# A two-layer decoder on one core: the last mixture writes finished rows, pads are cleared once counts are known, masks move to GpSimd

## The chip, the cores and the metric

The kernel runs as one program on one core of a Trainium2 chip. The engines of the core are named as the profile names them: PE is TensorE (PEld its weight loads), DVE is VectorE, ACT is ScalarE, POOL is GpSimd, and SP is SyncE, which here only starts DMAs. The metric is the device time of one execution in microseconds (us); less is better.

## The reference

The input x is 4 batches of 512 tokens with 128 features; a context of 154 tokens comes per batch. Two layers of attention and mixture follow, each added to x:

```python
x = x + L0_attn(layernorm(x), ...)            # linear attention
x = x + L0_xattn(layernorm(x), ctx, masks)    # 16 heads over 154 keys, two masks
x = x + L0_ffn(layernorm(x), ...)             # mixture: 8 experts, 1 chosen per token
x = x + L1_attn(layernorm(x), ...)            # relative positions
x = x + L1_xattn(layernorm(x), ctx, ...)      # causal over the keys
x = x + L1_ffn(x, ...)                        # rotary attention, then the mixture below
```

The last of them ends in the mixture that the change is mostly about:

```python
h = x + attention(rmsnorm(x, g1), wq, wk, wv, wo)
xf = rmsnorm(h, g2)                            # 2048 tokens x 128
vals, idx = top_k(xf @ router_w + router_b, 2)
scores = softmax(vals)
oh = one_hot(idx, 8)
pos = cumsum(cumsum(oh, axis=0), axis=1)       # place in the expert's queue
emask = oh * (pos < 256)
tmask = sum(emask, -1)
m = max(einsum('tke,e->tk', emask, arange(8)), -1)   # ONE expert per token
y = (gelu((xf @ w2[m]) * (xf @ w1[m])) @ w3[m])      # hidden size 256
out = h + sum_k scores_k * (y if tmask_k > 0 else xf)
```

So every token goes through exactly one expert m, and its result is `(h + xf * cz) + y * cy` with two factors per token, cz and cy, which are known before any expert has run.

## The kernel before, in words

The stages are named A to G in the code: A, B and C are the first layer's attention, cross-attention and mixture, D, E and F the second layer's attentions, G the last mixture. A, B and the gate of C run batch by batch, then C's experts, then D, then E, F and the gate of G batch by batch, then G's experts. Each engine has its own list of instructions, written out by hand in that order; semaphores are the only order between engines.

**Start.** SP issues the loads of the constants in groups; `s_const[1]` says that the second group (masks among it) has landed. In batch 0 the DVE normalises x, then runs `dve_prepare` (L709 to 723): it waits for that group and makes the bf16 masks `xmask`, `amask`, `kmask`, `cpick` and `cmask` and the column `pcol`. Only then come the values of the cross-attention (L569) and, when PE has projected x (L338), the keys of the linear attention `kf` (L386 to L390), for which PE waits (L346). L320 (the bias), L355 and L315 follow on PE. The masks are first read at L410 on DVE. POOL meanwhile widens the context's keys and values (L618, L621). SP also fills the scratch `xs_d` with zeros (L2022, 12.1 MB), since a mixture's tiles may hold rows that no token was written to.

**A mixture.** Tokens are grouped by expert through DRAM. An indirect DMA of POOL writes each group of 128 tokens to rows of `xs_d` (`pool_G_send`, L1829), each expert having a region. From the counts, `dve_tiles` (L835 to 857) works out which 23 tiles of 128 rows are to be run (NS = 23), the expert of each (`expert4`) and its first row (`rows4`). Then, for each tile s of the last mixture: SP loads the tile (L1938, six buffers); PE transposes it (`flip`, L1841) and DVE copies the result (L1902); POOL copies the two first weights of the tile's expert into one of two buffers (L1955); PE runs eight matmuls (`hidden`, L1850); ACT copies one half (L1882), DVE multiplies the halves (L1909), ACT applies Gelu (L1889); PE runs the third weight (`result`, L1860); DVE copies y out of PSUM (L1922); SP stores it over the tile's rows in `xs_d` (L1945). An instruction that takes a tile number or address from a table reads it first into a register (`value_load`).

When all tiles are stored, POOL gathers the rows back into token order with 16 indirect DMAs (L1960), DVE adds `y * cy` to `h + xf * cz` per batch (L1926), and SP writes the batch to the output (L2048).

**Between D and E.** SP stores D's last results, waits for them (`sp_D_store`), loads `rot` (L2039) and then `sp_D1` loads E's input in 18 DMAs per batch (L1410, L1415, L1416), for which POOL waits (L1431).

## Time and profile before

| what | us |
|---|---|
| median of 3 runs | 1671.35 |
| lowest and highest | 1669.7 and 1675.36 |
| the profiled execution's own time | 1675.38 |
| its span (first to last record) | 1673.6 |
| busy PE / DVE / ACT / POOL | 1423.6 / 966.6 / 749.0 / 232.3 |
| chain that ended last: PE / DVE / SP's queue / DMA / POOL | 69% / 15% / 4% / 3% / 2% |

The page gives busy time of each engine over the whole span, and the "chain that ended last", which is followed back from the last instruction to what released it. PE holds most of that chain, but not at its two ends. In the last 28 us, from 1646 on, PE and ACT have no instruction at all, and in the first 46 us the cores' clock for PE, shown as a granted share of full speed (1.0 is 2.4 GHz, 0.5 is 1.2 GHz), goes from one level to the other and back. A timeline row has the start, the duration, the engine, the line, the operation and its tiles, how many were merged, and in brackets how long the engine was idle before it and what ended that.

### The profile page before, as it was taken

To read this page: it belongs to the slowest core of one execution; us is meant where nothing else is said; L and a number is where in the kernel's file an instruction comes from. 1 tells how busy PE (TensorE), PEld (TensorE's weight loads), DVE (VectorE), ACT (ScalarE), POOL (GpSimd) and SP (SyncE) were. 2 spreads that over 40 slices of the span, in tenths; PEclk is the share of its full clock that TensorE was granted. 3 is DMA by queue.
4 is the path that set the end of the run, shared out by engine and by line. 5 is a ranking of instruction groups with operands and counts; after the bars stand their busy time and mean duration, and the time that the engine had idled before them with its cause. 6 is when DMAs were issued, how large, how long until landed. Compare 5 with 4: busy or idle time off the path is not lost.

```text
span 1673.6 us, 43831 instructions
## 1 busy us (share of the span) xinstructions
PE 1423.6 (85%) x17681; PEld 878.2 (52%) x17681; DVE 966.6 (58%) x2541; ACT 749.0 (45%) x1927; POOL 232.3 (14%) x201
## 2 busy tenths in 40 slices
PE   4889888696499999999958999889989898999672
PEld 3343434393266666766633466346644564456462
DVE  4354635323477777777723676576665776477532
ACT  1323142251266666666613276327723672447431
POOL 1011120123030030200010200030002100120124
PEclk7989999797799999999978899999989998899897
DMA  9600000023230100100021000000000000000012
GB/s 327 264 17 1 17 1 7 17 58 98 77 140 4 26 19 10 35 4 16 4 76 43 1 2 2 5 7 2 2 5 7 2 2 1 7 1 1 6 55 70
DMA packets 62072, 60.07 MB, mean 36 GB/s; under 512 B 27952, under 2 KB 47024, under 8 KB 60720
## 3 DMA queue, kind: packets, MB, share of 16 engines
q1 hardware_dynamic: 59536, 53.04, 10.0%
q0 software_dynamic: 2048, 4.20, 0.9%
q8 instruction: 142, 2.33, 0.6%
q14 instruction: 58, 0.48, 0.1%
q10 hardware_dynamic: 288, 0.03, 0.0%
HBM read 32.73 MB, written 24.51 MB: 34 GB/s over the span
## 4 chain that ended last, share of the span: by engine, by line
PE 69%; DVE 15%; issue 4%; SPq 4%; DMA 3%; ACT 3%; POOL 2%; ACTq 0%; POOLq 0%; DVEq 0%
PE ps L1126 7%; PE ps L1514 6%; PE ps L1533 5%; PE ps L500 5%; PE ps L1547 4%; PE ps L1106 4%; PE ps L1116 4%; DVE arena L586 4%; PE ps L1147 4%; PE ps L258 4%; PE ps L1502 3%; PE ps L474 3%; PE ps L1161 2%; PE ps L1556 2%; PE ps L797 2%
## 5 line engine op out<-in xcount | busy, mean ns | idle before, releaser
L1259 DVE TENSOR_REDUCE nmax<-ps 128x1 f32<-128x512 f32 x256 | 166.8, 683 | 56.3 <-PE ps L1116 55.7
L1590 ACT ACTIVATE arena<-ps,arena 128x512 f32<-128x512 f32 (+3 forms) x256 | 135.5, 531 | 119.1 <-DVE arena L1650 112.9
L1650 DVE TENSOR_REDUCE arena<-ps 128x1 f32<-128x512 f32 (+3 forms) x256 | 124.3, 487 | 78.8 <-PE ps L1518 76.7
L1219 ACT ACTIVATE arena<-ps,nmax 128x512 f32<-128x512 f32 x172 | 119.0, 692 | 80.8 <-DVE nmax L1259 79.3
L1533 PE MATMUL ps<-sqc,arena 128*128 128x128 f32 x640 | 106.6, 287 | 20.0 <-DVE arena L1658 19.7
L586 DVE TENSOR_REDUCE arena<-ps 128x8 f32<-128x1232 f32 x64 | 89.2, 1438 | 40.3 <-PE ps L462 40.1
L258 PE MATMUL ps<-identb 128*128 128x512 bf16 x408 | 110.0, 430 | 1.4 <-DVE kcol L707 1.4
L1267 DVE COPY arena<-ps 128x512 f32<-128x512 f32 x128 | 88.0, 688 | 39.9 <-PE ps L1126 38.4
L1514 PE MATMUL ps<-arena 64*128 64x384 f32 (+3 forms) x512 | 106.2, 493 | 0.0
L1658 DVE TENSOR_SCALAR arena<-arena 128x512 f32<-128x512 f32 (+3 forms) x256 | 100.8, 394 | 9.1
L598 DVE RECIPROCAL arena<-ps 128x128 f32<-128x128 f32 x8 | 7.7, 959 | 160.4 <-PE ps L500 160.4
L1547 PE MATMUL ps<-arena 128*64 128x128 f32 x1280 | 99.0, 286 | 0.0
L1601 ACT COPY arena<-ps 128x512 f32<-128x512 f32 (+3 forms) x256 | 95.8, 431 | 4.0 <-PE ps L1533 3.9
L1126 PE MATMUL ps<-sqc,arena 128*128 128x128 f32 x688 | 94.9, 281 | 2.1 <-DVE arena L1267 0.9
L1533 PEld LDWEIGHTS ps<-sqc,arena 128*128 128x128 f32 x640 | 71.9, 142 | 46.1 <-issue 26.4
L1126 PEld LDWEIGHTS ps<-sqc,arena 128*128 128x128 f32 x688 | 74.2, 142 | 21.4 <-issue 15.5
L1229 ACT COPY arena<-ps 128x512 f32<-128x512 f32 x128 | 74.4, 581 | 16.4 <-PE ps L1126 16.4
L1547 PEld LDWEIGHTS ps<-arena 128*64 128x64 f32 x1280 | 68.8, 138 | 13.6 <-issue 1.7
L1116 PEld LDWEIGHTS ps<-rk,cw 64*128 64x128 f32 x512 | 43.9, 190 | 60.0 <-issue 55.3
L258 PEld LDWEIGHTS ps<-identb 128*128 128x128 bf16 x408 | 45.3, 111 | 56.6 <-issue 22.5
L1116 PE MATMUL ps<-rk,cw 64*128 64x168 f32 (+25 forms) x512 | 74.6, 411 | 0.0
L306 ACT ACTIVATE root<-var 128x4 f32<-128x4 f32 x32 | 6.6, 206 | 148.6 <-DVE var L288 126.3
(350 smaller groups left out, 2713.1 us busy)
## 6 DMA issues: line engine op xcount, KB each, us to landing
xs_d<-onehot SPq DMA_DIRECT2D x3, 3072.0 KB, 29.6
cw<-in_cw SPq DMA_DIRECT2D x2, 2048.0 KB, 13.4
rv<-in_rv SPq DMA_DIRECT2D x2, 1536.0 KB, 19.7
late<-in_gw SPq DMA_DIRECT2D x3, 1024.0 KB, 10.8
arena<-xs_d SPq DMA_DIRECT2D x46, 64.0 KB, 1.8
xs_d<-arena SPq DMA_DIRECT2D x46, 64.0 KB, 1.6
xs_d<-onehot SPq DMA_DIRECT2D x1, 2560.0 KB, 22.4
onehot<-q_s SPq DMA_DIRECT2D x96, 8.0 KB
```

The costliest lines, as they stand in the source:

```text
L258: nc.tensor.matmul(ps[:, FILL[k][1], :].rearrange("p (a n) -> p a n", a=NT), identb[:, :], identb[:, :].unsqueeze(1).to_broadcast([P, NT, ...
L586: nc.vector.tensor_reduce(top_x[:, i, :, 2 * hp:2 * hp + 2], ps[:, bank:bank + NG4, 0:2 * KP].rearrange("p g (h k) -> p g h k", h=2)[:, :, ...
L1116: nc.tensor.matmul(ps[:, (4 * Q + j) % 5, k0:k1], AI[b % 2][64 * z:64 * z + 64, par * NW + w, :], rk[64 * z:64 * z + 64, r0:r0 + k1 - k0], ...
L1126: ins = nc.tensor.transpose(ps[:, TB[j % 2], i * P:(i + 1) * P], PB[k % 6][:, i * P:(i + 1) * P], c["ident"])
L1219: nc.scalar.activation(PB[k % 6], ps[:, k % 5, :], ACT.Exp, bias=nmax[:, u:u + 1], accum_out=rsum[:, b % 2, u:u + 1]).then_inc(SD["exp"], 1)
L1259: nc.vector.tensor_reduce(nmax[:, k % NU:k % NU + 1], ps[:, k % 5, :], AX.X, ALU.max, negate=True)\
L1514: nc.tensor.matmul(ps[:, FSB[n % 2][h], 0:wd], TF["q%d" % a][HALVES[h], i * P:(i + 1) * P], TF["kr%d" % (a % 2)][HALVES[h], 0:wd], start=T ...
L1533: ins = nc.tensor.transpose(ps[:, FTB[h], j * P:(j + 1) * P], TF["p%d" % (n % 2)][:, h * S + j * P:h * S + (j + 1) * P], c["ident"])
L1547: ins = nc.tensor.matmul(ps[HALVES[h], 4, i * P:(i + 1) * P], TF["v"][:, v0:v0 + KD], PTF[n % 2][h][:, j * P:(j + 1) * P], start=(j == 0), ...
L1590: nc.scalar.activation(TF["p%d" % (n % 2)][:, h * S:h * S + wd], ps[:, FSB[n % 2][h], 0:wd], ACT.Exp, bias=TF["nmax"][:, k4:k4 + 1], accum ...
L1650: nc.vector.tensor_reduce(TF["nmax"][:, k4:k4 + 1], ps[:, FSB[n % 2][h], 0:wd], AX.X, ALU.max, negate=True)\
L1658: nc.vector.tensor_scalar(TF["p%d" % (n % 2)][:, h * S:h * S + wd], TF["p%d" % (n % 2)][:, h * S:h * S + wd], TF["rinv"][:, k4], None, ALU ...
```

## The change

Four things change.

1. In the last mixture a token's row in DRAM becomes 258 wide: the normalised token (128), `h + xf * cz` (128), `cy`, and the token's own number (minus 4096). The rows live in a tile `G4` laid over the first mixture's weights and go to a scratch of their own, `gs_d`. DVE makes the finished row, y times `cy` plus the middle part, in one instruction out of PSUM, and POOL writes its 128 rows straight to the output by an indirect DMA whose index is the token's number plus 4096. A row of a tile that belongs to no token is all zero, so its index is 4096, beyond the output's 2048 rows, and is left out by the bounds check. The stores to `xs_d`, the 16 gathers, the 16 additions and the four output DMAs of G are gone.
2. Nothing of `gs_d` is zeroed beforehand, but for the last 128 rows. Once the counts are known, DVE works out the first row behind each expert's last token (`pad8`) and SP writes 128 zero rows there for each of the eight experts, before it loads the first tile. Regions shrink from 2560 to 2176 rows, and with them the zero fill of `xs_d` at the start (to 10.5 MB).
3. The copy of a tile's first two weights moves from POOL to ACT, with three buffers instead of two.
4. The masks of the start are made by POOL (`pool_prepare`) and not by DVE; `pcol` stays with DVE but moves behind B's normalisation. DVE waits for the masks at the instruction that reads them.

```diff
-REGION = 2560
+REGION = 17 * P
+GROWS = E1 * REGION + P
@@ dve_A, dve_X
             if b:
                 dve_C_choose(dve, ch, b - 1)
-            else:
-                dve_prepare(dve)
...
+            if b == 0:
+                dve.wait_ge(s_mask, 1)
             nc.vector.tensor_tensor(bmask, amask[:, :, 0:KP], ...
...
             if k == "B" and b == 0:
+                dve_prepare(dve)
                 dve_masks(dve)
@@ pool_prepare, called before selw is made
+        def pool_prepare(pool):
+            pool.wait_ge(s_const[1], 16 * len(GROUPS[1]))
+            nc.gpsimd.tensor_copy(xmask[:, :, 0:KP], xmask_in)
+            nc.gpsimd.tensor_copy(xmask[:, :, KP:KW], xmask_in[:, :, 0:KW - KP])
+            for mask, given in ((amask, amask_in), (kmask, kmask_in)):
+                nc.gpsimd.memset(mask[:, :, KS:KP], MASKED)
+                nc.gpsimd.tensor_scalar(mask[:, :, 0:KS], given[:, :, :], MASKED, None, ALU.mult)
+                ins = nc.gpsimd.tensor_scalar(mask[:, :, KP:KW], given[:, :, 0:KW - KP], MASKED, None, ALU.mult)
+            ins.then_inc(s_mask, 1)
+            nc.gpsimd.tensor_copy(cpick[:, :, :], causal_in[:, 0:2, :])
+            nc.gpsimd.tensor_copy(cmask[:, :, :], causal_in[:, 2:4, :]).then_inc(s_mask, 1)
@@ act_G
+            def weights(s):
+                e = act.value_load(expert4[0:1, s:s + 1], min_val=0, max_val=E2 - 1)
+                if s >= 3:
+                    act.wait_ge(SC["h"], NS + s - 2)
+                nc.scalar.copy(TG[f"w{s % 3}"]..., gw12[:, :, bass.ds(e, 1), :]...).then_inc(SC["w1"], 1)
...
             for s in range(NS):
+                if s + 2 < NS:
+                    weights(s + 2)
                 act.wait_ge(SG["p"], s + 1)
@@ dve_G
             dve.wait_ge(SG["count"], 1)
-            dve_tiles(ch, SG["table"])
+            V.scalar_tensor_tensor(pad8[:, :], ps[:, 0, 0:E2], 1.0, base8[:, :], ALU.add, ALU.add).then_inc(SG["pad"], 1)
+            dve_tiles(ch, SG["table"], GROWS - P)
...
-                    dve.wait_ge(SC_st[s % 4], 16 * (st_c[s % 4] + s // 4))
-                V.tensor_copy(TG[f"y{s % 4}"], ps[:, 6 + s % 2, 0:P]).then_inc(SC["yb"], 1)
-            for b in range(B):
-                dve.wait_ge(SC_yg[b], 2 * 16 * NT)
-                ...
+                    dve.wait_ge(SG_out[s % 4], 16 * (s // 4))
+                V.scalar_tensor_tensor(TG[f"y{s % 4}"], ps[:, 6 + s % 2, 0:P], XBG[s % NXB][:, 2 * P:2 * P + 1],
+                                       XBG[s % NXB][:, P:2 * P], ALU.mult, ALU.add).then_inc(SC["yb"], 1)
@@ sp_G
+            sp.wait_ge(SG["pad"], 1)
+            for e in range(E2):
+                r = sp.value_load(pad8[0:1, e:e + 1], min_val=0, max_val=GROWS - P)
+                sp.dma_start(gs_d[bass.ds(r, P), :], zero4).then_inc(SG["zero"], 16)
             sp.wait_ge(SC["sent"], 2 * 16 * NTT)
             sp.wait_ge(SG["table"], 1)
+            sp.wait_ge(SG["zero"], 16 * (E2 + 1))
+            for s in range(NS):
+                r = sp.value_load(rows4[0:1, s:s + 1], min_val=0, max_val=GROWS - P)
+                if s >= NXB:
+                    sp.wait_ge(SC["yb"], NS + s - NXB + 1)
+                    sp.wait_ge(SG["idx"], s - NXB + 1)
+                sp.dma_start(XBG[s % NXB], gs_d[bass.ds(r, P), :]).then_inc(SC_ld[s % NXB], 16)
@@ pool_G
             for s in range(NS):
+                pool.wait_ge(SC_ld[s % NXB], 16 * (ld_c[s % NXB] + s // NXB + 1))
+                if s >= 4:
+                    pool.wait_ge(SG_out[s % 4], 16 * (s // 4))
+                nc.gpsimd.tensor_scalar(gidx[:, s % 4:s % 4 + 1], XBG[s % NXB][:, 2 * P + 1:GW4], 2.0 * B * S, None, ALU.add)\
+                    .then_inc(SG["idx"], 1)
+                pool.wait_ge(SG["idx"], s + 1)
+                pool.wait_ge(SC["yb"], NS + s + 1)
+                nc.gpsimd.indirect_dma_start(out_rows, bass.IndirectOffsetOnAxis(ap=gidx[:, s % 4:s % 4 + 1], axis=0),
+                                             TG[f"y{s % 4}"], None, bounds_check=B * S - 1, oob_is_err=False)...
@@ SP, between D's stores and the load of rot
+            sp.wait_ge(s_own, 2)
+            sp.dma_start(gs_d[E1 * REGION:GROWS, :], zero4).then_inc(SG["zero"], 16)
@@ DVE, ahead of E: three small operations that fill the token numbers of G4
```

First place: DVE in batch 0 of the first stage, from the normalised x (`xn`) to the keys for PE (`arena` written from `tmp`). Before:

```order
L292 TENSOR_SCALAR xn<-arena,mv,rstd 128x128 x3
L712 CAST xmask<-arena 128x2x160 [waits s_const1]
L716 TENSOR_SCALAR amask<-arena 128x4x154
L717 TENSOR_SCALAR amask<-arena 128x4x96
L720 CAST cmask<-arena 128x256
L721 TENSOR_REDUCE pcol<-vmask 128x5
L723 TENSOR_SCALAR pcol<-pcol 128x5 [waits s_prep]
L386 TENSOR_TENSOR tmp<-ps,rowb 128x256 [waits s_akv]
L388 TENSOR_TENSOR arena<-ps,rowb 128x2x128 [waits s_ch0]
L390 TENSOR_SCALAR arena<-tmp,dec_col 128x128 x2
```

And now:

```order
L293 TENSOR_SCALAR xn<-arena,mv,rstd 128x128 x3
L570 TENSOR_TENSOR arena<-ps,rowb 128x640 [waits s_x_kv]
L385 TENSOR_TENSOR tmp<-ps,rowb 128x256 [waits s_akv]
L387 TENSOR_TENSOR arena<-ps,rowb 128x2x128 [waits s_ch0]
L389 TENSOR_SCALAR arena<-tmp,dec_col 128x128 x2
L411 TENSOR_TENSOR arena<-amask,kmask 128x640 [waits s_mask]
```

The wait for the second group of constants and the mask operations are no longer ahead of the keys on DVE; they stand on POOL, and DVE waits for them at L411.

Second place: POOL from the last send of tokens to its end. Before, of 23 alike only the last weight copies stand here:

```order
L1829 DMA xs_d<-rv,slot 23552x128 x3
L1952 TENSOR_LOAD expert
L1952 ISA x2
L1955 ISA [waits s_c_h]
L1955 COPY arena<-late 128x512
L1960 DMA rv<-xs_d,slot 128x128 [waits s_c_st2,s_c_st3,s_c_st1,s_c_st0]
L1960 DMA rv<-xs_d,slot 128x128 x15
```

And now, the first tiles of 23:

```order
L1842 DMA gs_d<-cw,slot 17536x258 x3
L1978 TENSOR_SCALAR g_idx<-arena 128x1 [waits s_c_ld0]
L1982 DMA out<-arena,g_idx 2048x128 [waits s_c_yb,s_g_idx]
L1978 TENSOR_SCALAR g_idx<-arena 128x1 [waits s_c_ld1]
L1982 DMA out<-arena,g_idx 2048x128 [waits s_c_yb,s_g_idx]
L1978 TENSOR_SCALAR g_idx<-arena 128x1 [waits s_g_out0,s_c_ld4]
```

The weight copies are gone from POOL; per tile it has one small operation and one indirect DMA, and nothing behind the last tile.

Third place: ACT in the same loop. Before (a tile has the two rows at the end):

```order
L1876 ACT_TABLE_LOAD
L1876 ACTIVATE warm<-sqc 128x1
L1882 COPY arena<-ps 128x256 [waits s_c_h]
L1889 ACTIVATE arena<-arena 128x256 [waits s_g_p]
L1882 COPY arena<-ps 128x256 [waits s_g_p,s_c_h]
L1889 ACTIVATE arena<-arena 128x256 [waits s_c_y,s_g_p]
```

And now, from the third tile on:

```order
L1895 COPY arena<-ps 128x256 [waits s_g_p,s_c_h]
L1898 TENSOR_LOAD expert
L1898 ISA x2
L1901 ISA [waits s_c_h]
L1901 COPY arena<-late 128x512
L1914 ACTIVATE arena<-arena 128x256 [waits s_c_y,s_g_p]
```

Between the copy of one half and Gelu stand now a register load and the copy of the weights.

## Rows read from the trace of the kernel before

**Rows 1.** the timeline of DVE at the start, batch 0.

```profile
19.93 1.40 DVE L717 TENSOR_SCALAR amask<-arena 128x384 bf16<-128x384 int32 x1
...
21.66 0.35 DVE L717 TENSOR_SCALAR kmask<-arena 128x384 bf16<-128x384 int32 x1
...
23.56 0.36 DVE L386 TENSOR_TENSOR tmp<-ps,rowb 128x256 f32<-128x256 f32 x1
```

**Rows 2.** the timeline of PE at the start, batch 0.

```profile
17.94 1.89 PE L338 MATMUL ps<-sqw,xnT 128*128 128x256 f32 x8
25.42 2.42 PE L346 MATMUL ps<-arena 128*128 128x144 f32 x8 [5.58 <-DVE arena L390]
27.76 2.07 PE L320 MATMUL ps<-rowb,sqc 1*128 1x512 f32 x2
29.76 2.29 PE L355 MATMUL ps<-arena 128*128 128x144 f32 x8
```

**Rows 3.** the timeline of batch 1 at the same place.

```profile
108.17 1.60 PE L346 MATMUL ps<-arena 128*128 128x144 f32 x8
...
110.41 1.12 PE L320 MATMUL ps<-rowb,sqc 1*128 1x512 f32 x2 [0.63 <-DVE slot L768]
...
111.46 1.25 PE L355 MATMUL ps<-arena 128*128 128x144 f32 x8
```

**Rows 4.** windows: busy by engine, then granted clock, DMA share, GB/s.

```profile
28.00:32.00 4.00, 4.00 (x10) 2.20 (x10) 0.25 (x2) 0.00 (x0) 0.00 (x0) 0.50 1.06 296
108.00:112.00 4.00, 3.26 (x17) 2.07 (x17) 3.03 (x13) 0.00 (x0) 1.33 (x1) 1.00 0.02 4
```

**Rows 5.** the timeline of all engines: POOL beside the masks, DVE's first use of them.

```profile
19.64 1.48 POOL L618 TENSOR_TENSOR arena<-arena,m 128x640 f32<-128x640 f32 x1
...
33.74 0.48 DVE L410 TENSOR_TENSOR arena<-amask,kmask 128x640 bf16<-128x640 bf16 x1
```

**Rows 6.** the timeline of the last mixture: the counts reach DVE.

```profile
1584.77 0.17 DVE L839 TENSOR_SCALAR c_cnt<-ps 128x8 f32<-128x8 f32 x1 [0.69 <-PE ps L1834]
```

**Rows 7.** the chain of waits ahead of the first tile: start, us, what.

```profile
1590.57 0.47 SPq L1935
```

**Rows 8.** SP's queue in the last mixture.

```profile
1591.50 5.82 SPq L1938 DMA_DIRECT2D arena<-xs_d  x6
...
1611.44 0.36 SPq L1945 DMA_DIRECT2D xs_d<-arena  x1
1612.55 0.33 SPq L1938 DMA_DIRECT2D arena<-xs_d  x1
```

**Rows 9.** the timeline of the last mixture: weight copies, first result, PE's tiles.

```profile
1589.28 1.30 POOL L1955 COPY arena<-late 128x512 f32 x2
...
1599.51 0.28 DVE L1922 COPY arena<-ps 128x128 f32<-128x128 f32 x1
...
1599.78 1.13 PE L1850 MATMUL ps<-arena 128*128 128x128 f32 x8 [0.24 <-DVE arena L1909]
...
1601.30 1.09 PE L1850 MATMUL ps<-arena 128*128 128x128 f32 x8
```

**Rows 10.** ACT in the loop, by groups: busy us, mean ns, idle.

```profile
L1889 ACT ACTIVATE arena<-arena 128x256 f32<-128x256 f32 x23 | 9.6, 417 | 13.5 <-DVE arena L1909 13.5
L1882 ACT COPY arena<-ps 128x256 f32<-128x256 f32 x23 | 8.6, 373 | 37.0 <-PE ps L1850 36.5
```

**Rows 11.** a copy of 512 columns on ACT, from the timeline.

```profile
16.34 0.59 ACT L270 COPY xnT<-ps 128x512 f32<-128x512 f32 x1 [3.37 <-PE ps L263]
```

**Rows 12.** the timeline behind the last tile: last result, gathers.

```profile
1645.36 0.29 DVE L1922 COPY arena<-ps 128x128 f32<-128x128 f32 x1 [1.05 <-PE ps L1860]
...
1649.54 0.96 POOL L1960 DMA_INDIRECT rv<-xs_d,slot  x1 [0.30 <-issue]
```

**Rows 13.** the chain of waits behind the last tile.

```profile
1647.47 0.77 issue
...
1667.07 2.33 DMA rv<-xs_d,slot
```

More of the change, by code:

```diff
@@ L189, in decoder @@
         s_prep = sem("s_prep")
+        s_mask = sem("s_mask")
         s_zero = sem("s_zero")
@@ L833, in act_C, with dve_tiles @@
                                          bias=colb[:, bass.ds(e * NC1 + (len(COLB) + j), 1)]).then_inc(SC["hs"], 1)
-        def dve_tiles(ch, done):
+        def dve_tiles(ch, done, limit):
             V = nc.vector
@@ L856, in dve_tiles @@
             ch(V.scalar_tensor_tensor(s_row[:, :], s_e[:, :], float(REGION), s_t[:, :], ALU.mult, ALU.add))
-            V.tensor_copy(rows4[:, :], s_row[:, :]).then_inc(done, 1)
+            V.tensor_scalar(rows4[:, :], s_row[:, :], float(limit), None, ALU.min).then_inc(done, 1)
         def dve_C(dve, ch):
@@ L1686, in pool_F @@
                     .then_inc(SF["qr"], 1)
-        SG = {n: sem("s_g_" + n) for n in ("gate", "d", "e2", "oh", "cum", "seen", "pick", "rank", "slot", "count", "table", "a", "p")}
+        SG = {n: sem("s_g_" + n) for n in ("gate", "d", "e2", "oh", "cum", "seen", "pick", "rank", "slot", "count", "table", "a", "p", "zero", "idx", "pad")}
+        SG_out = [sem("s_g_out%d" % i) for i in range(4)]
         ld_c, st_c = ([len(range(z, NS, n)) for z in range(n)] for n in (NXB, 4))
@@ L1695, in decoder @@
         used[0] = 0
-        XBG = [cut(P) for _ in range(NXB)]
-        TG = dict(**{f"xT{z}": cut(P) for z in range(2)}, **{f"w{z}": cut(2 * HID2) for z in range(2)},
+        GW4 = 2 * P + 2
+        G4 = cw[:, 0:NTT * GW4].rearrange("p (t n) -> p t n", n=GW4)
+        XBG = [cut(GW4) for _ in range(NXB)]
+        g_p = sb("g_p", [P, 1])
+        pad8 = sb("g_pad", [P, E2], mybir.dt.int32)
+        gidx = sb("g_idx", [P, 4], mybir.dt.int32)
+        gs_d = nc.dram_tensor("gs_d", (GROWS, GW4), F32, kind="Internal").ap()
+        out_rows = out.rearrange("b s d -> (b s) d")
+        TG = dict(**{f"xT{z}": cut(P) for z in range(2)}, **{f"w{z}": cut(2 * HID2) for z in range(3)},
                   **{n + str(z): cut(HID2) for n in "aph" for z in range(2)}, **{f"y{z}": cut(P) for z in range(4)})
         TG.update(oh=sb("g_oh", [P, NT * 2 * E2])[:, :], cum=sb("g_cum", [P, NT * 2 * E2])[:, :], sum=sb("g_sum", [P, 2 * E2])[:, :])
-        cy4 = sb("g_cy", [P, NTT])
-        tiles_of = lambda a, b: a[:, b * S:(b + 1) * S].rearrange("p (i n) -> p i n", i=NT)
-        yn4, xo4, yg4 = (lambda b, a=a: tiles_of(a, b) for a in (own4, x4, other4))
+        yn4, xo4 = (lambda b, k=k: G4[:, b * NT:(b + 1) * NT, k * P:(k + 1) * P] for k in range(2))
+        cy4 = lambda b: G4[:, b * NT:(b + 1) * NT, 2 * P]
         gw12 = late[:, sum(LATE[:4]):sum(LATE[:6])].rearrange("p (m e n) -> p m e n", m=2, e=E2)
@@ L1827, in pool_G_send @@
             pool.wait_ge(SG["slot"], b + 1)
-            for n in range(NT):
-                nc.gpsimd.indirect_dma_start(xs_d, bass.IndirectOffsetOnAxis(ap=slot4[:, b * NT + n:b * NT + n + 1], axis=0),
-                                             yn4(b)[:, n, :], None).then_inc(SC["sent"], 16)
+            for n in range(b * NT, b * NT + NT):
+                nc.gpsimd.indirect_dma_start(gs_d, bass.IndirectOffsetOnAxis(ap=slot4[:, n:n + 1], axis=0),
+                                             G4[:, n, :], None).then_inc(SC["sent"], 16)
         def pe_G(pe):
@@ new lines, in sp_G, with sp_G_pad @@
+                    sp.wait_ge(SG["idx"], s - NXB + 1)
+                sp.dma_start(XBG[s % NXB], gs_d[bass.ds(r, P), :]).then_inc(SC_ld[s % NXB], 16)
+            for z in range(4):
+                sp.wait_ge(SG_out[z], 16 * st_c[z])
+        zero4 = kmask[:, :, :].rearrange("p b n -> p (b n)").bitcast(F32)[:, 0:GW4]
+        def sp_G_pad(sp):
+            sp.wait_ge(SG["pad"], 1)
+            for e in range(E2):
+                r = sp.value_load(pad8[0:1, e:e + 1], min_val=0, max_val=GROWS - P)
+                sp.dma_start(gs_d[bass.ds(r, P), :], zero4).then_inc(SG["zero"], 16)
@@ L2045, in _ @@
             sp_G(sp)
-            for b in range(B):
-                sp.wait_ge(s_xout, b + 1)
-                sp.dma_start(out[b:b + 1].rearrange("o (t p) d -> p (o t) d", p=P), xo4(b)).then_inc(s_store, 16)
-            sp.wait_ge(s_store, B * 16)
         @block.tensor
@@ L2135, in _ @@
             ch.turn(0)
+            ch(nc.vector.tensor_reduce(g_p[:, 0:1], c["tri"], AX.X, ALU.add))
+            ch(nc.vector.tensor_scalar(g_p[:, 0:1], g_p[:, 0:1], -1.0, float(P - 2 * B * S), ALU.mult, ALU.add))
+            ch(nc.vector.tensor_scalar(G4[:, :, 2 * P + 1], row["index"][:, 0:NTT], float(P), g_p[:, 0:1], ALU.mult, ALU.add))
             for b in range(B):
```

75 lines of the change are left out of this document (24 added, 51 removed).

## The prediction

> **What bounds the kernel now.** I read the chain of waits first: PE carries 69% of it, so most of the span is not touched by an edit that leaves PE's work alone. Then I read the timeline at the two places where the change lies and where PE is not what ends the wait. At the start PE waits 5.58 us for DVE before L346, and DVE was making masks until shortly before the keys (L386 at 23.56) [rows 1, 2]. Behind the last tile nothing computes: the last result is copied at 1645.36 + 0.29 = 1645.65, and the span ends at 1673.6, 27.95 us later, which is one chain of 16 gathers on POOL, each 0.96 with 0.30 between, a landing of 2.33, an addition and an output DMA [rows 12, 13]. In the loop over the 23 tiles SP's queue sets the pace: it alternates load and store about 1.11 apart, so 2.22 per tile [rows 8]. While its first six loads were still ahead of the work, PE went from one tile's eight matmuls to the next in 1601.30 - 1599.78 = 1.52 [rows 9].
>
> **The start.** Nothing is removed here; the mask work moves from DVE to POOL. DVE can begin the keys when the first half of L338 is done, about 17.94 + 0.95 = 18.9, plus 0.1 for the semaphore, so at 19.0 and not at 23.56: 4.5 us earlier [rows 1, 2]. On top of it comes PE's clock. L346, L320 and L355 took 2.42 + 2.07 + 2.29 = 6.78 in batch 0 and 1.60 + 1.12 + 1.25 = 3.97 in batch 1, a difference of 2.8; the granted clock was 0.50 in the first case and 1.00 in the second (1.2 and 2.4 GHz), and what went before was 5.6 us of idle PE in the first and continuous work in the second [rows 2 to 4]. With the wait cut to under 2 us I expect most of it at the high level, worth up to 2.8. Against this stands contention: L717 took 1.40 for `amask` and 0.35 for `kmask`, the same shape, and the slow one lay across POOL's L618 (19.64 to 21.12) [rows 1, 5]. POOL now runs its mask operations just while DVE makes the keys, so each of the two pairs of L390 may wait for a POOL operation, 0 to 1.05 each, 0 to 2.1 in all; I take 1.3, a little over half, as POOL is busy most of that time. Sum: 4.5 + 2.8 - 1.3 = 6.0 gained, between 2.4 (no clock) and 7.3 (no contention).
>
> The Trainium skill, SBUF — State Buffer, section "SBUF: two separate sides", has a rule that speaks against this part: VectorE and GpSimd share one pair of ports under an exclusive lock, held for a whole instruction. By that rule the gain is the sum with all four key operations held up, so nearer the low end; the pair of L717 rows agrees with it, with 1.05 us as the price of one.
>
> Do the masks come in time? DVE reads them at 33.74 before, so at about 27.7 now [rows 5]. POOL starts them when the constants land at 18.7. No such operation of POOL is in the trace; its copy of 512 f32 columns is 0.65 [rows 9], its two-input L618 over 640 is 1.48 [rows 5]. There are 2512 columns ahead of the signal (320 + 192 + 2 x (616 + 384)): at copy rate 3.2, at L618's rate 5.8. I take 4.5, near the copy since all have one input: done at 23 to 25, under cover by 3 us. If it took over 9 us, the rest would come out of the gain. `pcol` (0.5) moves to where DVE waits for PE's first flipped mask and costs 0 to 0.5; I take 0. The smaller zero fill is on no wait of this stretch: 0.
>
> **Between D and E.** SP issues one more DMA ahead of `rot` and E's loads, behind which POOL waits: 0.33 to 0.36 of issue [rows 8], so 0.4 lost, 0 to 1.0. Three small DVE operations run while E's loads are under way: 0. POOL's sends have rows of 1032 bytes instead of 512; they are off the path but for the last four, and those end before the pads below: 0.
>
> **The pads, ahead of the first tile.** The counts reach DVE at 1584.77; one operation more gives `pad8` at about 1584.95 [rows 6]. From the end of its last wait to its first DMA SP needed 1591.50 - 1590.57 = 0.93, and six loads took 5.82, 0.97 each with their register reads [rows 7, 8]. So the first pad is issued at 1585.9, the eighth at 1585.9 + 7 x 0.97 = 1592.7. SP must wait for it to land: 2.0, an estimate a little below the 2.33 that POOL's last gather took to land [rows 13], since SP's own queue issues it; 1.5 or 2.5 would move the sum by 0.5. Loads may start 0.93 behind, at 1595.6 and not 1591.5. Each load is twice as large: 0.3 more. So the first tile is 4.4 later (3 to 5.5), and its result (1599.51 + 0.28 = 1599.8 before) is ready at 1604.2 [rows 9]. What is queued behind the wait is all of SP's loads, and for these wait PE, DVE and POOL.
>
> **The loop.** SP has only loads left: about 1.0 per tile, no bound. PE can do 1.52 [rows 9]. ACT gets the weight copy. Per tile: 0.42 + 0.37 [rows 10], a copy of 512 columns 0.59 [rows 11], and a register read. Of SP's 0.97, 0.33 is the DMA, so the read is about 0.63; POOL hid such a read wholly behind a copy (two copies in 1.30) [rows 8, 9]. ACT's own 0.37 hides part of it, 0.26 is left: 1.64, with gaps of 0.04 between four instructions 1.75 to 1.8. With nothing hidden 0.42 + 0.37 + 0.59 + 0.63 plus gaps is 2.2. POOL's part is an index operation (unseen, 0.1 to 0.4), a start of 0.30 to 0.77 and the scatter of 0.96 [rows 12, 13]: 1.4 to 2.1. I take 1.8 per tile, close to ACT's sum, with 1.52 and 2.3 as ends. DVE's operation on y becomes one with three inputs, 0.28 to 0.4; DVE has under 1.2 per tile, no bound. The six load buffers are now held until y is done; a load takes about 3 us from there, and its tile is wanted three tiles (5.4) later: 0.
>
> **The end.** The last result is at 1604.2 + 22 x 1.8 = 1643.8. Then POOL starts the last scatter (0.3), it lands 2.33 later [rows 13], and 0.4 go by until the end: 1646.8, against 1673.6. Gained 26.8; with 1.52 per tile 33, with 2.3 per tile 15.8.
>
> **The sum** on the profiled execution: 1675.38 - 6.0 + 0.4 - 26.8 = 1643.0. That execution was 4.0 above the median shown, so for the median: 1671.35 - 32.4 = 1638.95, told as 1639.
>
> **Rivals.**
> - *An engine becomes the bound of the loop, at about 2.3 per tile.* For it: ACT with an unhidden register read comes to 2.2, and a POOL scatter behind its own index operation and a semaphore may need 2.1 or more. Against it: POOL's read was hidden, and gathers ran at 1.26. The loop costs 22 x 0.5 = 11 more: 1650.
> - *The gain of the start is lost*, to the port, or since POOL's masks are late (over 9 us of work), and PE's clock falls anyway. For it: the 1.05 of L717. Left is 0 to 1 of 6.0: 1644.
> - *PE alone bounds the loop* (1.52): 22 x 0.28 = 6.2 less: 1633.
> - *Slower: the scatters are serial.* Place: POOL's loop. If the index operation behind a scatter can start only when that scatter has landed, a tile costs 2.33 + 0.77 + 0.2 + 0.3 = 3.6 and the loop 22 x 1.8 = 39.6 more: 1679. It ends on the slower side from 1.8 + 32.4 / 22 = 3.27 per tile. Against it: POOL's weight copy began at 1589.28, when the last send had ended on POOL but not landed (SP's wait for it ended at 1590.57) [rows 7, 9].
>
> The Trainium skill has a price for a like mechanism in the same section: a DMA that GpSimd issues takes about 0.62 us alone and 3.1 beside a VectorE copy from SBUF to SBUF, since its descriptors wait for the port. By it a tile could cost over 3.3, and that is this last rival's side of the forecast. DVE's operations in this loop read PSUM, and no row here shows such a delay.
>
> **How the numbers follow.** Forecast with 1.6 to 2.0 per tile and a start between 4 and 7.3: 0.56, 1639, own range 1633 to 1645. Loop bound by another engine: 0.25, 1650. Start lost: 0.11, 1644. PE's bound: 0.04, 1633. Serial scatters: 0.03, 1679. The last 0.01 is no change at all. The range 1631 to 1651 leaves out the scatters and the upper part of the loop rival. Within 0.3% (5 us, about what a measurement of this kernel can tell from no change) would need 27 us of the 32 to be missing. Faster 0.95, same 0.02, slower 0.03.
>
> **What would show it.** In the profile after: L346 starting near 20 to 21 and the granted clock still high beneath L355; POOL's masks ending before DVE's first use of them at about 28, with no idle DVE there; eight DMAs on SP from 1580 on (all times are some 5.6 earlier by then) and the first load 4 later than before, counted from the counts; 1.8 per tile between PE's groups of eight; no POOL work after the last result but one scatter, and an end about 3 us behind it. The forecast is wrong if the tiles are more than 2.1 apart, if DVE waits for masks, or if PE at the start stays at 1.2 GHz.

## The result, and the profile after

| | before | changed | forecast |
|---|---|---|---|
| median | 1672.73 (4 runs) | 1650.81 (4 runs) | 1639, range 1631 to 1651 |
| span of the profiled execution | 1673.6 | 1652.9 | 1641.2 (1643.0 less the 1.8 around the span) |
| ratio, 95% interval | | 0.9871 (0.984 to 0.9903) | 0.981 |
| start of DVE's first operation on the counts (`c_cnt`) | 1584.77 | 1576.27 | 1579.2 |
| from there to the end of the span | 88.8 | 76.6 | 62.0 |

The change is faster by 1.3%, 22 us, where 32 were forecast. The median lies within 0.2 us of the upper end of the range, 12 us above the forecast. The last two lines of the table divide the miss. Up to the counts the kernel gained 8.5 us (forecast 5.6), behind them 12.2 (forecast 26.8). The first is better than forecast by 3, the second worse by 14.6.

**The start.** The timeline of the changed kernel in batch 0; a row has start, duration, engine, line, operation, and in brackets the idle time before it:

```profile
19.11 1.78 POOL L718 TENSOR_SCALAR amask<-arena 128x616 bf16<-128x616 int32 x1
19.11 1.89 PE L339 MATMUL ps<-sqw,xnT 128*128 128x256 f32 x8
20.18 0.42 DVE L385 TENSOR_TENSOR tmp<-ps,rowb 128x256 f32<-128x256 f32 x1 [5.02 <-PE ps L339]
...
20.98 0.77 DVE L389 TENSOR_SCALAR arena<-tmp,dec_col 128x128 f32<-128x128 f32 x2
...
21.69 0.73 PE L347 MATMUL ps<-arena 128*128 128x144 f32 x4 [0.69 <-DVE arena L389]
...
22.45 0.89 DVE L389 TENSOR_SCALAR arena<-tmp,dec_col 128x128 f32<-128x128 f32 x2
...
23.89 1.12 PE L321 MATMUL ps<-rowb,sqc 1*128 1x512 f32 x2
24.18 1.17 POOL L719 TENSOR_SCALAR kmask<-arena 128x384 bf16<-128x384 int32 x1
24.94 1.25 PE L356 MATMUL ps<-arena 128*128 128x144 f32 x8
...
27.87 0.54 DVE L411 TENSOR_TENSOR arena<-amask,kmask 128x640 bf16<-128x640 bf16 x1
```

The keys begin at 20.18 (forecast 19.0; 23.56 in [rows 1]); POOL's masks end at 24.18 + 1.17 = 25.35, and DVE does not wait for them at L411 (27.87). L321 and L356 take 1.12 and 1.25 as in [rows 3], not 2.07 and 2.29 as in [rows 2]. The windows show how long PE stayed at the lower granted clock (busy time by engine, then granted clock, DMA share, GB/s). Before:

```profile
28.00:48.00 20.00, 13.58 (x83) 9.54 (x84) 9.68 (x37) 4.61 (x9) 0.00 (x0) 0.50 1.03 384
```

And after:

```profile
24.00:28.00 4.00, 2.77 (x13) 1.63 (x13) 2.08 (x9) 0.00 (x0) 3.88 (x7) 1.00 0.99 409
28.00:36.00 8.00, 4.25 (x40) 3.81 (x40) 7.16 (x27) 3.79 (x8) 1.81 (x2) 0.62 1.04 362
36.00:40.00 4.00, 2.57 (x35) 1.77 (x34) 1.34 (x4) 0.82 (x2) 0.00 (x0) 0.90 0.99 384
```

The clock record has 0.50 (1.2 GHz) from 24.5 to 48.4 before (so a little beyond the first 46 us named above), and from 30.0 to 36.8 in this execution: 24 us have become seven. So the gain grows from 3.4 at the keys to 8.4 at PE's L442 (L443 now), which began at 51.32 and begins at 42.95.

**The last mixture.** First the pads and the first tile, from the timeline (SPq is SP's queue, its duration covers all DMAs of the row):

```profile
1576.19 0.17 DVE L1921 SCALAR_TENSOR_TENSOR g_pad<-ps,c_base 128x8 int32<-128x8 f32 x1 [0.69 <-PE ps L1847]
...
1577.32 8.37 SPq L1971 DMA_DIRECT2D gs_d<-kmask  x8
...
1588.13 12.03 SPq L1961 DMA_DIRECT2D arena<-gs_d  x8
...
1597.01 0.35 DVE L1948 SCALAR_TENSOR_TENSOR arena<-ps,arena 128x128 f32<-128x128 f32 x1
```

The first result is ready at 1597.01 + 0.35 = 1597.36, 21.1 behind the counts; it was forecast to be ready 19.4 behind them (1604.2 - 1584.77). Then the end of the loop:

```profile
1641.42 0.35 DVE L1948 SCALAR_TENSOR_TENSOR arena<-ps,arena 128x128 f32<-128x128 f32 x1 [0.99 <-PE ps L1873]
1641.47 1.06 POOL L1982 DMA_INDIRECT out<-arena,g_idx  x1 [0.79 <-POOL g_idx L1978]
...
1643.61 1.06 POOL L1982 DMA_INDIRECT out<-arena,g_idx  x1 [0.79 <-POOL g_idx L1978]
1644.74 0.21 POOL L1978 TENSOR_SCALAR g_idx<-arena 128x1 int32<-128x1 f32 x1
1645.74 1.06 POOL L1982 DMA_INDIRECT out<-arena,g_idx  x1 [0.79 <-POOL g_idx L1978]
```

DVE's results come (1641.42 - 1597.01) / 22 = 2.02 apart, POOL's last scatters 1645.74 - 1643.61 = 2.13. POOL's first scatter starts at 1598.27, so that all 22 turns have a mean of 2.16, slower than the results throughout. POOL's turn is 0.21 of index, 0.79 idle before its own index operation counts as done and the scatter starts, 1.06 of scatter and 0.07. When the last result is ready, POOL is in one scatter and still has two to do. And behind the last one there are 6 us in which no engine computes. What holds them is in the instructions of POOL's queue at the program's end (duration in ns, start), after and then before:

```profile
L93 POOLq DRAIN  x1: 7174/7174/7174, 1645.5 to 1645.5; - x1
```

```profile
L92 POOLq DRAIN  x1: 18189/18189/18189, 1655.1 to 1655.1; - x1
```

POOL's closing drain ends at 1645.5 + 7.17 = 1652.7, 6.9 behind the start of the last scatter, though that one had landed after 2.2. Before it ended at 1673.3, 6.2 behind the start of the last gather [rows 13], and was hidden: the addition and the output DMA took as long.

### The profile page after: what moved, and what is told of

The parts are those of the page before. It is cut to its first block, busy times and chain, and to the rows that moved or that the text cites. A ratio compares the mean times of both kernels' runs of the same rounds, so it can differ in the third digit from the quotient of the medians.

```text
span 1652.9 us, 43828 instructions
## 1 busy us (share of the span) xinstructions
PE 1418.1 (86%) x17669; PEld 874.9 (53%) x17681; DVE 960.3 (58%) x2519; ACT 761.2 (46%) x1950; POOL 239.5 (14%) x219
## 3 DMA queue, kind: packets, MB, share of 16 engines
q8 instruction: 142, 2.33, 0.6%
## 4 chain that ended last, share of the span: by engine, by line
PE 71%; DVE 15%; issue 4%; ACT 3%; DMA 2%; SPq 2%; POOL 2%; ACTq 0%; POOLq 0%; DVEq 0%
PE ps L1132 7%; PE ps L1520 6%; PE ps L1539 5%; PE ps L501 5%; PE ps L1553 4%; PE ps L1112 4%; PE ps L1122 4%; PE ps L1153 4%; DVE arena L588 4%; PE ps L259 4%; PE ps L1508 3%; PE ps L475 3%; PE ps L1167 2%; PE ps L1562 2%; PE ps L803 2%
## 5 line engine op out<-in xcount | busy, mean ns | idle before, releaser
L1235 ACT COPY arena<-ps 128x512 f32<-128x512 f32 x128 | 74.4, 581 | 14.5 <-PE ps L1132 14.3
L1122 PEld LDWEIGHTS ps<-rk,cw 64*128 64x128 f32 x512 | 44.2, 191 | 60.0 <-issue 55.3
## 6 DMA issues: line engine op xcount, KB each, us to landing
cw<-in_cw SPq DMA_DIRECT2D x2, 2048.0 KB, 13.2
```

The lines of the kernel that those rows point to most:

```text
L1122: nc.tensor.matmul(ps[:, (4 * Q + j) % 5, k0:k1], AI[b % 2][64 * z:64 * z + 64, par * NW + w, :], rk[64 * z:64 * z + 64, r0:r0 + k1 - k0], ...
```

## The experiments

Eleven kernels. The medians of the kernel before differ between sets (1670.57 to 1676.34), and the six kernels that are alike up to the counts reach them at 1567.1 to 1582.3 of their profiled executions, 15 us apart. So each term is read from a trace, between two places of one execution, and the ratio says whether the whole agrees. "Counts to end" begins with `c_cnt`, DVE's first operation on the counts proper; the expectations count from the one for the pads ahead of it, 0.1 earlier. "D's last store to E's first sum" goes from the start of SP's last DMA of D's results to the start of POOL's first addition of E.

| kernel | ratio to before (95%) | PE at L442 | D's last store to E's first sum | counts to end |
|---|---|---|---|---|
| before | 1 | 51.3 | 13.2 | 88.8 |
| changed | 0.9871 (0.984, 0.9903) | 43.0 | 14.9 | 76.6 |
| masks only | 0.9956 (0.9933, 0.9979) | 44.0 | 12.5 | 89.1 |
| tail only | 0.9938 (0.991, 0.9966) | 51.1 | 14.7 | 76.5 |
| index ahead | 0.9826 (0.9787, 0.9864) | 46.3 | 14.6 | 72.4 |
| PE's read moved | 0.9878 (0.9841, 0.9915) | 44.9 | 14.4 | 76.0 |
| both | 0.9813 (0.977, 0.9857) | 44.0 | 14.5 | 67.1 |
| last two scatters out | (one run, 1654.36) | 43.5 | 15.0 | 72.5 |
| pads on two queues | 0.9868 (0.9811, 0.9925) | 44.2 | 14.4 | 75.6 |
| gs_d zeroed in D | 1.0087 (1.0051, 1.0123) | 44.9 | 13.2 | 71.2 |
| both, zeroed in D | 1.0059 (1.0028, 1.0089) | 42.6 | 13.3 | 62.8 |
| gs_d zeroed in E | 0.9862 (0.9825, 0.9899) | 44.3 | 13.0 | 71.2 |
| both, zeroed in E | 0.9778 (0.9746, 0.9811) | 43.4 | 12.9 | 62.6 |

**Index ahead of the scatter (on the changed kernel).**

```diff
+            index(0)
             for s in range(NS):
-                (wait for the load, index of s, wait for it)
+                if s + 1 < NS:
+                    index(s + 1)
+                pool.wait_ge(SG["idx"], s + 1)
                 pool.wait_ge(SC["yb"], NS + s + 1)
                 nc.gpsimd.indirect_dma_start(out_rows, ...)
```

> The changed kernel, with one edit: POOL makes the index of tile s+1 before it scatters tile s, so that it no longer waits for an operation of its own that it has just issued. Theory 1 (the 0.79 us between the index operation's end and the scatter is that wait plus the scatter's start): POOL's turn falls from 2.14 us to about 1.65 (scatter 1.06, gap 0.07, index 0.21, start 0.3), POOL is no longer behind, and PE's pace of 2.02 us per tile sets the loop. The last scatter then starts about 0.3 us after the last result instead of 4.0 after it: time 1647.1 us against 1650.8 of the changed kernel (ratio to before 0.985). Theory 2 (any scatter that follows another kind of POOL instruction starts 0.8 us late): POOL stays at 2.1 us per tile and the time at 1650.8.

Measured: median 1644.95, counts to end 72.4. POOL's timeline there:

```profile
1643.41 0.21 POOL L1978 TENSOR_SCALAR g_idx<-arena 128x1 int32<-128x1 f32 x1
1643.92 1.06 POOL L1987 DMA_INDIRECT out<-arena,g_idx  x1 [0.30 <-issue]
...
1646.41 0.35 DVE L1948 SCALAR_TENSOR_TENSOR arena<-ps,arena 128x128 f32<-128x128 f32 x1 [1.09 <-PE ps L1873]
1647.62 0.98 POOL L1987 DMA_INDIRECT out<-arena,g_idx  x1 [0.39 <-issue]
```

Where the result is already there, a scatter starts 0.30 behind an index operation of another tile, not 0.79. The other 0.49 was the wait for its own result. POOL now follows DVE, the scatters are (1647.62 - 1604.15) / 22 = 1.98 apart, and the last starts 1.2 behind the last result's start instead of 4.3. Theory 1 holds; 4.2 us of the missing 14.6 were POOL's.

**PE's register read behind the eight matmuls.**

```diff
             def hidden(s):
-                e = nc.tensor.value_load(expert4[0:1, s:s + 1], ...)
                 ...
                 ins.then_inc(SC["h"], 1)
-                return e
+                return nc.tensor.value_load(expert4[0:1, s:s + 1], ...)
```

> The changed kernel, with one edit: PE reads a tile's expert number into a register behind the eight matmuls of hidden and not ahead of them (only the third weight needs it). Theory 1 (POOL at 2.14 us per tile bounds the end; PE's 2.0 per tile is 1.5 of work and a register read of 0.4 that nothing covers): PE runs at 1.6 to 1.9 us per tile until it is held back by the four result buffers, the last scatter doesn't move, time 1650.8 us, within 1. Theory 2 (POOL merely follows PE and the result): 22 tiles x 0.3 = 6.6 less, 1644 us.

Measured: median 1651.79, and 76.0 against 76.6. Theory 1 holds: alone it brings almost nothing. PE's rows show why:

```profile
1613.30 0.33 PE L1854 MATMUL ps<-sqc,arena 128*128 128x128 f32 x1 [0.75 <-DMA arena<-gs_d]
1613.47 1.06 PE L1862 MATMUL ps<-arena 128*128 128x128 f32 x8
...
1615.40 0.33 PE L1854 MATMUL ps<-sqc,arena 128*128 128x128 f32 x1 [0.40 <-DMA arena<-gs_d]
```

PE now waits for loads, because a load buffer is free only when POOL has read its index, and POOL is late. The slow engine at the end of the line holds the first one through the six load buffers, not through the four result buffers as I had written.

**Both edits.**

> Both edits on the changed kernel: the index one tile ahead on POOL, PE's register read behind hidden. Theory 1: what is left as pace is ACT (0.37 + 0.28 + 0.62 + 0.41 = 1.68 us of its own per tile, with waits 1.8 to 1.9), so the last scatter starts at about 1638.3 of the span instead of 1645.7: time 1643.4 us (range 1641 to 1645), ratio 0.983. Theory 2 (the loop of hidden, linear, product, Gelu, result has a latency of 2.0 per tile of its own): 1647, as with the index alone.

Measured: median 1639.28, counts to end 67.1, results 1.75 apart (1591.4 to 1629.8). Theory 1's direction holds and its size was too careful: 7.5 was expected to go behind the counts, 9.6 went. How PE's series changed is seen in its weight loads of the changed kernel:

```profile
1618.97 0.97 PEld L1863 LDWEIGHTS ps<-arena 128*128 128x128 f32 x8 [0.47 <-issue]
1619.96 0.52 PEld L1873 LDWEIGHTS ps<-late,arena 128*128 128x128 f32 x4
1620.40 0.14 PEld L1854 LDWEIGHTS ps<-sqc,arena 128*128 128x128 f32 x1
1620.98 0.97 PEld L1863 LDWEIGHTS ps<-arena 128*128 128x128 f32 x8 [0.43 <-issue]
```

and in the matmuls of this kernel:

```profile
1610.79 0.27 PE L1854 MATMUL ps<-sqc,arena 128*128 128x128 f32 x1
1610.90 1.06 PE L1862 MATMUL ps<-arena 128*128 128x128 f32 x8
1611.79 0.62 PE L1872 MATMUL ps<-late,arena 128*128 x4
1612.24 0.27 PE L1854 MATMUL ps<-sqc,arena 128*128 128x128 f32 x1
1612.35 0.83 PE L1862 MATMUL ps<-arena 128*128 128x128 f32 x6
```

In the first fence PE is never short of data. It has 1.63 of weight loads in series, and 0.43 to 0.47 in which its queue reads a register and nothing covers it: 2.0. In the second a turn without a wait is 1.45 (1610.90 to 1612.35). The mean stays at 1.75; in 12 of the turns PE waits for ACT's Gelu, 4.5 us in all. Whether ACT's work or the round from PE over ACT and DVE back to PE sets the 1.75 is not settled. With POOL out of the way in both kernels, moving the read takes the pace from 1.98 to 1.75. Not every read costs the same: with the index ahead alone, every second turn has 0.44 to 0.51 in this place and the others 0.08 to 0.16.

**The masks alone, and all but the masks.** The first kernel is the one before with `pool_prepare` and its waits as in the diff of the change. The second is the changed kernel with `dve_prepare` as before.

> The kernel before, with the masks of the start made by POOL and nothing else changed. Theory 1 (the start's gain is from this part alone: keys 3.4 us earlier, and 5.0 more because PE spends 7 us and not 23 at the lower granted clock): the first stage's PE runs 8.4 us earlier from 45 us on, time 1664.3 us against 1672.7 (ratio 0.995). Theory 2 (the clock's part came from elsewhere, such as the smaller zero fill): 3.4 to 6 us, 1667 to 1669. Theory 3 (the gain is given back to the clock later): 1671, ratio 0.999.

> The changed kernel with its masks made by DVE again as before, so that only the last mixture, the pads and the smaller zero fill are left of the change. Theory 1 (start and tail are two separate gains, 8.4 us of the start and 12.1 of the tail in the two profiled executions): the start is as before, the stretch from the counts to the end stays at 76.7 us, time 1672.7 - 12.1 = 1660.6 us, ratio 0.993. Theory 2 (the start's gain is lost on the way by the clock, and the tail or the smaller fill carries all): 1651 to 1654, ratio 0.988.

Measured: 1665.56 and 1661.18. PE reaches L442 at 44.0 in the first and at 51.1 in the second, so the masks are the whole of the start's gain, clock included. In the eleven kernels that have them on POOL it is 5.0 to 8.7 us, each from one execution. The part of the clock is what differs: the low stretch lasted 24 us in the two kernels with the masks on DVE, and 7 us in three of the eleven, 10 in five, 14 in two and 20 in one (index ahead, where the keys came 4.5 us earlier and PE reached L442 only 5.0 earlier). So seven, as in the changed kernel, is the best case and not the rule. What makes the clock fall sooner or later among kernels with the same start was not tested. In the tail-only kernel the window from 28 to 48 is that of before:

```profile
28.00:48.00 20.00, 13.58 (x84) 9.32 (x84) 9.43 (x35) 4.61 (x9) 0.00 (x0) 0.50 1.03 384
```

Theory 1 of both expectations holds for the times and for the stretch behind the counts. In the kernel with the masks alone PE spent 10 us at the lower clock and not the 7 it named, and the gain at L442 is 7.3 and not 8.4. The two ratios give 0.44% + 0.62% = 1.1% together, against 1.3% for the change, within the intervals.

**The last two scatters left out.** `range(NS - 2)` in `pool_G`, and SP's last waits to match.

> The changed kernel with the scatters of the last two of 23 tiles left out (up to 256 rows of the output are not written), nothing else. The last scatter then starts about 65.3 us after the counts, the last result is made 65.4 after them. Theory 1 (the program ends when POOL's drain does, 6.9 us after the start of the last indirect DMA, whoever else is done): end 65.3 + 6.9 + 0.2 = 72.4 us after the counts, against 76.7 of the changed kernel. Theory 2 (the last 5 us come from SP's wait for the scatter's landing or from something fixed at the end of any program): 69 us, as the landing takes 2.2.

Measured: counts to end 72.5, theory 1's 72.4. The last result was there at 1645.05 + 0.35, and the last scatter started at 1645.56:

```profile
1645.05 0.35 DVE L1948 SCALAR_TENSOR_TENSOR arena<-ps,arena 128x128 f32<-128x128 f32 x1 [1.09 <-PE ps L1873]
1645.56 1.06 POOL L1982 DMA_INDIRECT out<-arena,g_idx  x1 [0.79 <-POOL g_idx L1978]
```

```profile
L93 POOLq DRAIN  x1: 7004/7004/7004, 1645.3 to 1645.3; - x1
```

The end moved with the last indirect DMA: the drain ended 6.8 behind its start, 6.9 in the changed kernel. What POOL does in these microseconds the trace doesn't show.

**Pads on two queues.** ACT issues four of the eight, SP the others.

```diff
+            act.wait_ge(SG["pad"], 1)
+            pads(act, range(1, E2, 2))
```

> The changed kernel with four of the eight pads issued by ACT and four by SP. Theory 1 (the pads' price is the issue: a register read and a DMA, 1.05 us each, one after the other on one queue): last issue 4 us earlier, first load about 4 us earlier, the stretch from the counts to the end 72.7 us against 76.7, time 1646.8. Theory 2 (the price is the transfer of 1.03 MB in rows of 1 KB and its landing): 1 us or less.

Measured: median 1651.77, counts to end 75.6, one less. The issue shrank as expected, from 8.37 to 3.85, but the landing grew. The DMA groups of the two kernels (KB each, median us from issue to landing), this one and then the changed kernel:

```profile
gs_d<-kmask ACTq DMA_DIRECT2D x4, 129.0 KB, 4.2
gs_d<-kmask SPq DMA_DIRECT2D x4, 129.0 KB, 4.5
```

```profile
gs_d<-kmask SPq DMA_DIRECT2D x8, 129.0 KB, 2.4
```

Theory 2 is nearer: behind the issue stands the transfer, 1.06 MB of pads beside 0.53 MB of tokens that POOL sends at that moment. SP still waited 4.9 for it.

**gs_d zeroed beforehand, no pads.**

```diff
-            sp_G_pad(sp)
...
+            dst = gs_d.rearrange("(p r) d -> p r d", p=P)[:, a:a + n, :]
+            sp.dma_start(dst, zero4.unsqueeze(1).to_broadcast([P, n, GW4])).then_inc(SG["zero"], 16)
```

> The changed kernel, but all of gs_d (18.1 MB) is zeroed beforehand, in four DMAs that SP issues beside stage D, where the page shows the DMA engines 5 to 20% busy, and the eight pads behind the counts are gone. Theory 1 (the pads stand on the path with their whole length, eight issues of 1.05 us and a landing): the first tile is loaded 5.8 us after the counts, as before, instead of 11.9, and the stretch from the counts to the end falls from 76.7 to 70.6 us; time 1644.7 us, ratio to before 0.983. Theory 2 (the loop has slack that absorbs it, since POOL's backlog is what counts): the stretch falls by less than 2 us. A loss of its own could be that D's loads stand in the queues behind the fill: then D is longer by the same measure, and the stretch behind the counts is not.

> Index one tile ahead, PE's register read behind hidden, and gs_d zeroed beside stage D instead of the pads. Theory 1 (the three terms add, since they are in series): from the counts to the end 67.1 - 6.1 = 61.0 us, time 1633 us (1631 to 1636), ratio 0.977. Theory 2 (the earlier start is taken up elsewhere): 64 to 67 us and 1637 to 1640.

Measured: 1691.15 and 1685.76, slower than before. Behind the counts the time fell as expected (71.2 and 62.8), so the pads cost 5.4 and not the 6.1 expected. But D's last store came 44 to 49 us later than in the changed kernel. SP's queue, PE's longest stops and the window of D:

```profile
464.40 1.42 SPq L2035 DMA_DIRECT2D late<-in_gw  x3
465.86 26.99 SPq L1970 DMA_DIRECT2D gs_d<-kmask  x2
```

```profile
499.85 1.90 PE L1112 MATMUL ps<-tmp,arena 32*32 32x512 f32 x11 [4.41 <-issue]
510.75 1.33 PE L1132 MATMUL ps<-sqc,arena 128*128 128x128 f32 x5 [4.10 <-issue]
```

```profile
470.00:520.00 50.00, 33.76 (x735) 22.00 (x732) 21.25 (x35) 20.11 (x50) 7.45 (x3) 0.90 1.09 221
```

PE is busy for 33.8 of these 50, against 49.2 in the changed kernel. A mean DMA share of a tenth had seemed room enough. I had named a loss of this kind, D's loads behind the fill, and put no number on it, but the rows don't show that one: the loads in SP's queue stand ahead of the fill, and SP's queue was free again at 492.9, long before its next DMA, a store at 576.5. What they show is PE standing still for 3.2 to 4.4 us at a time, four times between 486 and 521, without a wait that the profile can name ("issue"), while the fill keeps the DMA engines' share at 1.09. What PE stood for there is open.

**The same zeroing in stage E.** The four DMAs stand behind `sp_D1`'s loads.

> The zeroing of gs_d beforehand again, but issued by SP behind the loads of stage E's inputs (from 900 us on, where the page shows the DMA engines at 1% for 180 us) and not beside stage D, where it held up D's loads. No pads behind the counts. Theory 1 (its cost in stage D was only the queue in front of D's own loads): nothing waits for it now, the counts come when they do in the changed kernel, and from the counts to the end it takes 71.2 us as with the first zeroing, against 76.6: time 1645.4 us, ratio to before 0.984. Theory 2 (18.1 MB of writes slow PE's or DVE's stages wherever they are, or the write of it isn't done when the first tokens are sent): 1651 or more.

> Index one tile ahead on POOL, PE's register read behind hidden, and gs_d zeroed in stage E. Theory 1 (the three terms add): from the counts to the end 62.8 us, as the same edits had with the zeroing in stage D; time 1635 us, ratio 0.979 (0.976 to 0.981). Theory 2 (the zeroing costs in stage E what it cost in D, 45 us): over 1670.

Measured: 1648.28 and 1635.20. Counts to end 71.2 and 62.6, as in stage D, and nothing that could be seen is lost on the way. SP's queue:

```profile
891.16 53.72 SPq L1969 DMA_DIRECT2D gs_d<-kmask  x4
945.23 95.58 SPq L2017 DMA_DIRECT2D ctxT<-in_ctxT  x4
```

The times and stretches are theory 1's for both. Its reason, the queue in front of D's loads, is not borne out by the rows of stage D above. It isn't the load on the DMA engines alone either: from 891 to 950 their share is 1.09 here too, and PE is busy for 53.5 of these 59 us and has no stop as in D, with 258 matmuls against 735 in D's 50 us. The last is the fastest version of all, 2.2% under the kernel before, and by the two ratios 0.9% under the changed one. As a single edit the zeroing can't be told from the changed kernel by the ratios (0.9862 and 0.9871), only by the stretch in the trace.

The column in the middle of the table holds one more term. In every kernel that issues the 129 KB DMA of zeros ahead of `rot`, E's first sum comes 14.4 to 15.0 behind D's last store; in the six kernels without it 12.5 to 13.3. SP's row of E's first loads shows most of that, before and after:

```profile
859.06 7.19 SPq L1415 DMA_DIRECT2D rv<-y_s  x16
```

```profile
853.97 8.49 SPq L1421 DMA_DIRECT2D rv<-y_s  x16
```

One DMA ahead costs its own 0.35, and the sixteen behind it are issued 1.3 more slowly. In the seven kernels with that DMA the sixteen take 8.0 to 8.5, in the six without it 6.7 to 7.3.

## Why the prediction was wrong in size

The direction was right, and so were the mechanisms of the start and of the pads. Two steps of the sum behind the counts failed. The larger is the loop: "I take 1.8 per tile, close to ACT's sum", where POOL needed 2.16 and PE 2.0. The other is the end: 0.3, 2.33 and 0.4 behind the last result, with POOL's closing drain of 7 us put at nothing. The stretch behind the counts was forecast at 62.0 and took 76.6. The difference has four parts (they add up to 14.6 before rounding):

| step of the prediction | it said | measured | us |
|---|---|---|---|
| first result ready, behind the counts | 19.4 | 21.1 | +1.7 |
| results of 22 tiles | 1.8 apart | 2.02 | +4.8 |
| from the last result to the last scatter's start | 0.3 | 4.0 | +3.7 |
| from there to the end | 2.7 | 7.2 | +4.5 |

- **The pace of the loop (+4.8).** "PE can do 1.52" was read from one pair of groups at the very start of the loop [rows 9]. The groups of eight that follow in the same trace are these:

```profile
1603.53 1.13 PE L1850 MATMUL ps<-arena 128*128 128x128 f32 x8 [0.23 <-DVE arena L1909]
1605.05 1.08 PE L1850 MATMUL ps<-arena 128*128 128x128 f32 x8
```

So the turns were 1.52, 2.23 and 1.52, and by PE's weight loads the eight turns from there on have a mean of 1.94: the pair was the short half of an alternation, and the trace of before already had a pace near 2.0 (what held its long turns was not separated). The changed kernel's turn is 2.0 with an uncovered register read in it. The experiment with both edits takes it to 1.75, below the 1.8 of the forecast. ACT, which I took as the bound at 1.8, was idle for 0.36 to 0.49 in the turns looked at, waiting for PE.

- **POOL (+3.7).** The term was bounded about rightly (1.4 to 2.1 per tile) and its upper end was true: 2.13 a turn, 2.16 as a mean. The step that failed is to take 1.8, "close to ACT's sum", for the loop as a whole while POOL's bound, and PE's turns, lay above it. In the changed kernel POOL alone sets the end, and the two rows of the table together are its delay: with only PE's read moved, the stretch shrank by 0.6. The experiment with the index ahead takes 4.2 us out again and leaves PE's pace. The first rival, an engine at about 2.3 per tile, 1650, was the case that came, with POOL as the engine. That its time fits to 1 us is luck in part: the pace was below 2.3, and the drain, which it didn't have, made up for it.
- **The end (+4.5).** "It lands 2.33 later and 0.4 go by" names the landing and not POOL's drain. The row of the drain was in the trace before, hidden to within 0.3 us: SP's queue waited that long at the end. I had read the chain, in which it doesn't appear, and not the instructions of the last line. This is a wait that took the place of the one removed, and no rival had it.
- **The pads (+1.7 in the first result).** Cost in all: 5.4 (the stretch without them) against the 4.4 of the forecast. The first pad was issued 1.13 behind the operation that gives `pad8`, and the last landed in 2.0, both about as forecast, but seven steps took 8.04 and not 6.8: 1.15 each, for 0.97 between loads. The rest, 0.6, lies behind the first load: the granted clock of the four microseconds in which the second group of matmuls ran was 0.66, against 0.87 before.
- **The start (better by 2.4).** DVE began the keys 1.2 later than forecast, because PE's projection did, and two costs in the sum were wrong in opposite directions. The clock was priced on three groups of matmuls at 2.8, but the low stretch before went on to 48 and also held L315 (2.08, now 1.21) and fourteen matmuls of L258 (4.52, now 3.19): from the keys to L442 the gain grew by 5.0. That size is luck in part, as the other kernels show: with the index ahead the same stretch gave 0.5. The contention was priced at 1.3 on top of what was there, but the two pairs of L390 took 1.17 and 0.47 before and 0.77 and 0.89 after, 1.64 against 1.66: nothing was added, since the kernel before already paid it. By the Trainium skill (page "SBUF — State Buffer", section "SBUF: two separate sides") the engine that starts first holds the shared ports for its whole instruction and the other is blocked, when VectorE's operation is in a two-port mode or has two inputs in SBUF. Whether L390 is of that kind the trace doesn't say. The 1.17 of before fits: its first operation ended 0.1 behind POOL's L621. The pairs of the changed kernel don't: they ended 0.4 and 0.8 before the POOL operation that they ran beside, and in the two kernels zeroed in stage E all four took 0.28, the last two wholly within a POOL operation of 1.8 us. Where the wait did show was L411, which has two such inputs: 1.80 and 1.85 us in two kernels in which it started together with POOL's L623, 0.54 in the changed one.
- **Masks in time: right.** 7.1 us of POOL and not 4.5, above the upper bound of 5.8, but done 2.5 before they are read.
- **D to E (+1.3).** 0.4 was taken, 1.0 was the bound, 1.7 is what the column shows.
- **Serial scatters: excluded.** An index operation starts 0.07 behind a scatter's end, never at its landing. The Trainium skill's 3.1 us for a DMA that GpSimd issues beside a VectorE copy (same page and section) is not seen: all 23 scatters took 1.06, with DVE busy beside them. DVE's operations there read PSUM, so the Trainium skill's own case, a copy from SBUF to SBUF, was not tested.

Of the 8.5 us at the counts, 8.4 come from the start and 1.7 are lost between D and E; the other 1.8 lie in stages that the change doesn't touch, well within the 15 us by which kernels that are alike there differ. What makes single executions drift in these stages was not tested.

## What to carry to other kernels

When an edit takes a long serial tail away, look for what was running beside that tail and ended just under it: here POOL's closing drain, 7 us behind its last indirect DMA, was covered before to within 0.3 us. A loop's pace is the largest of its engines' full turns, with every register read and every wait for an engine's own last operation in it, measured over many turns in the steady state and not on one pair. And each engine's bound has to be set beside the others before one value is taken for the loop.
